# Storing the first attention's normalised rows as f16 high and low halves, and turning those halves in the first expert stage

## The reference

```python
x = x + tanh(g_xattn[0]) * attention(layernorm(x), ctx, ...)      # causal, one head
x = x + tanh(g_ffn[0]) * experts(layernorm(x), Wr, W1, b1, W2, b2, ...)
# experts: 8 experts, 2 per token, at most 640 tokens for each
probs = softmax(xn @ Wr.T); scores, chosen = top_k(probs, 2); scores /= scores.sum(-1)
for e in range(8):
    idx = the first 640 tokens that chose e (and did not overflow earlier)
    y[idx] += (gelu(xn[idx] @ W1[e] + b1[e]) @ W2[e] + b2[e]) * score[idx]
# tokens past an expert's 640 are computed by a fallback network instead
x = x + tanh(g_xattn[1]) * dilated_attention(...)                 # second layer, not touched
x = x + tanh(g_ffn[1]) * expert_choice(...)
```

## Time and profile before

| | us |
|---|---|
| three runs | 849.19, 846.90, 848.25 |
| median | 848.25 |
| the profiled execution | 846.92 |
| span of its instructions | 845.2 |
| mean granted clock of TensorE | 0.869 of full speed |

### The profile page before, as it was taken

One profiled execution on the slowest core, in us unless ns is written; L12 is line 12 of the kernel. 1 busy time (PEld: TensorE's weight loads), 2 busy tenths in 40 slices (PEclk: granted clock), 3 DMA queues, 4 the chain that ended last, 5 costly groups with the idle time before them and its releaser, 6 DMA issues. The chain is left out here.

```text
span 845.2 us, 14866 instructions
## 1 busy us (share of the span) xinstructions
PE 634.7 (75%) x4843; PEld 473.2 (56%) x4843; DVE 513.2 (61%) x1772; ACT 415.3 (49%) x810; POOL 345.8 (41%) x478
## 2 busy tenths in 40 slices
PE   6998898289999999999523778877977730158994
PEld 5787786248768767877411445544544420046773
DVE  1575666666666575564106667779775618866752
ACT  2444431165785686577111466556755611046772
POOL 2433343465347337542312443344533312034754
PEclk9998999679999999999855798889988955569999
DMA  5461233355464455542311222223200014015643
GB/s 162 145 201 51 76 103 123 85 155 145 89 143 105 95 124 113 140 79 27 49 51 32 59 77 65 71 69 91 86 33 28 26 39 150 0 59 145 153 109 38
DMA packets 73873, 75.95 MB, mean 90 GB/s; under 512 B 8037, under 2 KB 66449, under 8 KB 73553
## 3 DMA queue, kind: packets, MB, share of 16 engines
q1 hardware_dynamic: 61217, 59.32, 22.7%
q0 software_dynamic: 10928, 15.57, 11.0%
q10 hardware_dynamic: 1664, 0.27, 0.2%
HBM read 52.20 MB, written 22.94 MB: 89 GB/s over the span
## 5 line engine op out<-in xcount | busy, mean ns | idle before, releaser
L1896 DVE CUSTOM_DVE_ANT_0 c_sn<-c_ps_s,k_mask 128x128 f32<-128x128 f32 (+1 forms) x256 | 75.8, 352 | 55.0 <-PE c_ps_s L2034 54.8
L1420 PE MATMUL b_ps_y<-b_w2h,b_hh 128*128 128x256 f16 x320 | 87.3, 273 | 4.7 <-DVE b_xl L1313 4.4
L1230 POOL DMA_INDIRECT res<-b_y,b_s_idx x40 | 73.4, 1834 | 41.6 <-ACT b_y L1272 31.8
L1728 POOL TENSOR_SCALAR_AFFINE_SELECT c_pr<-c_pr 128x512 f32<-128x512 f32 x64 | 42.8, 669 | 110.0 <-ACT c_pr L1787 109.0
L1420 PE MATMUL b_ps_y<-b_w2h,b_hl 128*128 128x256 f16 x320 | 87.2, 273 | 0.0
L1420 PE MATMUL b_ps_y<-b_w2l,b_hh 128*128 128x256 f16 x320 | 87.2, 273 | 0.0
L1304 DVE TENSOR_TENSOR b_hl<-b_h,b_hh 128x640 f16<-128x640 f32 x64 | 52.9, 826 | 39.2 <-ACT b_hh L1252 39.0
L1216 POOL DMA_INDIRECT e_xg<-rows,e_g_idx x35 | 36.9, 1056 | 83.5 <-DVE e_g_idx L1331 73.0
L2062 PE MATMUL c_ps_v<-c_pr,k_vx 128*64 128x256 f32 (+1 forms) x512 | 64.3, 378 | 5.5 <-POOL c_pr L1728 4.8
L1385 PE MATMUL b_ps_h<-b_xh,e_w1h 128*128 128x320 f16 x256 | 57.1, 305 | 3.1 <-ACT b_h L1247 2.1
L1787 ACT ACTIVATE c_pr<-c_ps_t 128x768 f32<-128x768 f32 x64 | 51.7, 807 | 13.8 <-PE c_ps_t L2048 13.8
(11 more groups left out here) (400 smaller groups left out, 1768.1 us busy)
## 6 DMA issues: line engine op xcount, KB each, us to landing
e_w<-in_L_ffn_W_dram SPq DMA_DIRECT2D x16, 1024.0 KB, 5.5
d_w<-in_L_ffn_W_down_dram SPq DMA_DIRECT2D x8, 640.0 KB
k_ks<-kT SPq DMA_DIRECT2D x48, 64.0 KB, 2.9
c_qs<-q SPq DMA_DIRECT2D x48, 64.0 KB, 2.3
d_w<-in_L_ffn_W_up_dram SPq DMA_DIRECT2D x4, 682.0 KB, 5.3
rows<-a_rows SPq DMA_DIRECT2D x8, 264.0 KB, 2.8
rows<-c_rows SPq DMA_DIRECT2D x8, 264.0 KB, 2.2
a_x_in<-in_x_dram SPq DMA_DIRECT2D x8, 256.0 KB, 3.5
```

Source lines behind the costliest of these rows:

```text
L1230: pool.indirect_dma_start(out=dram["res"], out_offset=bass.IndirectOffsetOnAxis(ap=s_idx[u][:, j:j + 1], axis=0), in_=y[:, j, :], in_offse ...
L1420: last = pe.matmul(ps_y[(j + CT) % 2][:, 0:D], a, b[:, f, :], start=(f == 0 and k == 0), stop=(f == FC - 1 and k == 2))
L1728: pool.affine_select(out=late, in_=late, compare_op=ALU.is_ge, fill=0.0, base=0, pattern=[[0, 2], [0, 2], [1, P]], channel_multiplier=-1). ...
L1896: dve.tensor_tensor_reduce(sn[r][:, a:b], ps_s[:, r, a:b], mask[:, a:b], -1.0, 3.0e38, ALU.add, ALU.min, mx[g % 2][:, q, r, j:j + 1]).then ...
```

## The change

The tile `rows` keeps its size, but its first 256 f32 words of a row now hold 256 f16 high halves and then 256 f16 low halves; the 8 gate weights stay f32. ACT normalises into a new f32 tile `x1n`, copies that to the high half, and POOL subtracts the high half from `x1n` for the low half, in `gates_of`, between the match table and the weighted one-hots. PE turns `x1n` for the router as it turned `rows`. SP's store of the rows waits for both halves in place of the normalised rows. In the expert stage PE turns high and low halves with an f16 identity, two transposes each, into f16 parts of the same bank; ACT copies the high part and DVE copies the low part. The overflow programs add the halves.

```diff
+def row_parts(tile, D):
+    flat = tile[:].bitcast(F16)
+    return flat[..., 0:D], flat[..., D:2 * D]
...
+        x1n = [sb(f"x1n{u}", [P, 2, D]) for u in range(2)]
+        rows_hi, rows_lo = zip(*(row_parts(r, D) for r in rows))
...
             def gathered(g, u):
-                after(sp, s_xn1, g, 0, 2)
+                after(sp, s_rhi, g)
+                after(sp, s_rlo, g)
                 after(sp, s_gate, g, 0, 2)
...
             pool.memset(ident[:], 0.0).then_inc(s_cst, 1)
+            pool.memset(keep["ident16"][:], 0.0).then_inc(s_ecst, 1)
...
+            pool.affine_select(out=keep["ident16"][:], in_=keep["ident16"][:], compare_op=ALU.not_equal, fill=1.0,
+                               base=0, pattern=[[-1, P]], channel_multiplier=1).then_inc(s_ecst, 1)
...
                 landed(pool, s_rst, g, u, 2)
+                after(pool, s_rhi, g)
+                pool.tensor_tensor(rows_lo[u], x1n[u][:], rows_hi[u], ALU.subtract).then_inc(s_rlo, 1)
                 after(pool, s_pg, g, 0, 2)
...
             def residual_normalised(m, v):
+                after(act, s_x1, m, 0, 2)
+                after(act, s_px1, m, 2)
+                after(act, s_rlo, m, 2)
+                normalise(m, s_nmr1, rstd1[v], nmr1[v], x1[v], x1n[v], s_xn1)
                 landed(act, s_rst, m, v, 2)
-                after(act, s_x1, m, 0, 2)
-                normalise(m, s_nmr1, rstd1[v], nmr1[v], x1[v], rows[v], s_xn1)
+                after(act, s_xn1, m, 0, 2)
+                act.activation(rows_hi[v], x1n[v][:], ACT.Copy).then_inc(s_rhi, 1)
...
-                turn(ps_x, rows[u]).then_inc(s_px1, 1)
+                turn(ps_x, x1n[u]).then_inc(s_px1, 1)
...
-        ps_x = [ps_y[k][:, 0:C * P].rearrange("p (c t) -> p c t", c=C) for k in range(2)]
+        x_parts = [[part.rearrange("p (c t) -> p c t", c=C) for part in row_parts(ps_y[k], D)] for k in range(2)]
...
-                        act.activation(xh[v][:, :, j * P:(j + 1) * P], ps_x[j % 2], ACT.Copy).then_inc(s_xh, 1)
+                        act.activation(xh[v][:, :, j * P:(j + 1) * P], x_parts[j % 2][0], ACT.Copy).then_inc(s_xh, 1)
...
                         dve.wait_ge(s_xh, (e + 1) * CT + j + 1)
-                        dve.tensor_tensor(xl[v][:, :, j * P:(j + 1) * P], ps_x[j % 2],
-                                          xh[v][:, :, j * P:(j + 1) * P], ALU.subtract).then_inc(s_xl, 1)
+                        dve.tensor_copy(xl[v][:, :, j * P:(j + 1) * P], x_parts[j % 2][1]).then_inc(s_xl, 1)
...
-                        for c in range(C):
-                            last = pe.transpose(ps_x[j % 2][:, c, :], xg[v][:, j, c * P:(c + 1) * P], ident[:])
+                        for to, part in zip(x_parts[j % 2], row_parts(xg[v], D)):
+                            for c in range(C):
+                                last = pe.transpose(to[:, c, :], part[:, j, c * P:(c + 1) * P], keep["ident16"][:])
                         last.then_inc(s_px, 1)
```

More of the change, by code:

```diff
@@ L256, in attention_causal @@
         s_mr1 = sem("mr1"); s_nmr1 = sem("nmr1")
-        s_xn1 = sem("xn1"); s_px1 = sem("px1"); s_x1T = sem("x1T"); s_plg = sem("plg")
+        s_xn1 = sem("xn1"); s_rhi = sem("rhi"); s_rlo = sem("rlo"); s_px1 = sem("px1"); s_x1T = sem("x1T"); s_plg = sem("plg")
         s_lg = sem("lg"); s_top = sem("top"); s_tix = sem("tix"); s_tixf = sem("tixf"); s_dl = sem("dl")
@@ L408, in _ @@
                       allow_small_or_imprecise_dtypes=True).then_inc(s_ecst, 1)
-            pool.wait_ge(s_ecst, 7)
+            pool.wait_ge(s_ecst, 8)
+            pool.affine_select(out=keep["ident16"][:], in_=keep["ident16"][:], compare_op=ALU.not_equal, fill=1.0,
+                               base=0, pattern=[[-1, P]], channel_multiplier=1).then_inc(s_ecst, 1)
             pool.affine_select(out=tri[:], in_=tri[:], compare_op=ALU.is_ge, fill=0.0, base=0,
@@ L774, in _ @@
             values(2)
-            dve.wait_ge(s_ecst, 8)
+            dve.wait_ge(s_ecst, 10)
             dve.tensor_copy(free[:], one_row[:]).then_inc(s_free, 1)
@@ L1009, in _ @@
             values(4)
-            pe.wait_ge(s_ecst, 8)
+            pe.wait_ge(s_ecst, 10)
             pe.wait_ge(s_ldb1, 16)
@@ L1435, in overflow_programs @@
     fg = sb("f_fg", [P, NT])
-    rows = sb("f_rows", [P, S.ROW]); res = sb("f_res", [P, D])
+    rows = sb("f_rows", [P, S.ROW]); xr = sb("f_xr", [P, D]); res = sb("f_res", [P, D])
     xT = sb("f_xT", [P, C, P]); h = sb("f_h", [P, FC, P])
@@ L1440, in overflow_programs @@
     s_xT = sem("f_xT"); s_ph = sem("f_ph"); s_h = sem("f_h"); s_py = sem("f_py"); s_yb = sem("f_yb")
-    s_y = sem("f_y"); s_new = sem("f_new"); s_store = sem("f_store"); s_passs = sem("f_passs")
+    s_y = sem("f_y"); s_new = sem("f_new"); s_xr = sem("f_xr"); s_store = sem("f_store"); s_passs = sem("f_passs")
     rows_t = dram["rows"].rearrange("(t p) d -> t p d", p=P)
@@ L1481, in on_vector @@
             with dve.Fori(0, NT) as i:
+                dve.wait_ge(s_rows, (i + 1) * 16)
+                hi, lo = row_parts(rows, D)
+                dve.tensor_tensor(xr[:], hi, lo, ALU.add).then_inc(s_xr, 1)
                 dve.wait_ge(s_py, i + 1)
@@ L1494, in on_tensor @@
             with pe.Fori(0, NT) as i:
-                pe.wait_ge(s_rows, (i + 1) * 16)
+                pe.wait_ge(s_xr, i + 1)
                 for c in range(C):
-                    last = pe.transpose(ps_x[:, c * P:(c + 1) * P], rows[:, c * P:(c + 1) * P], ident[:])
+                    last = pe.transpose(ps_x[:, c * P:(c + 1) * P], xr[:, c * P:(c + 1) * P], ident[:])
                 last.then_inc(s_px, 1)
@@ L2674, in build @@
             ("prob", [P, S.NT, S.E]), ("fallen", [P, S.NT]))}
+        keep["ident16"] = ctx.enter_context(nc.sbuf_tensor("ident16", [P, P], F16))
         keep["fallen_n"] = ctx.enter_context(nc.sbuf_tensor("fallen_n", [P, 1], I32))
```

## The result

The changed kernel takes 858.37 us (median of 4 runs) where the kernel before took 847.58 beside it: a ratio of 1.0123, with a 95% interval of 1.0087 to 1.0158. That is 10.8 us slower. The forecast was 856.3, 8.1 slower. Two executions of the kernel before, taken beside hi_alone_filled, both_fill and before_fill_wait, lasted 1276.50 and 3138.58 us and are in no median and no ratio. The profiled executions stand 11.2 apart (858.17 against 846.92, spans 856.4 and 845.2), and these 11.2 are not where the forecast had them. I cut both spans at four points of PE: the first and the last start of the router's logits (line 941, now 959), the first turn of the experts (line 1396, now 1414), and the first and the last start of the second expert product (line 1420, now 1438).

What follows compares the result with a forecast made beforehand. It took the block pipeline as a chain round the engines and the expert stage as PE's own length plus waits. 4.5 + 3.0 + 1.2 + 1.6 + 0 - 2.2 = +8.1 gave 856.3 us, range 850.5 to 861.0.

Steps and rivals of the forecast that it cites:

- its own last test: Forecast called wrong if pipeline start-to-start times don't grow, or the expert stage gains more than 4 us.
- The high half on ACT: Block pipeline: one more copy between normalised rows and exponentials, 0.65 in each of seven blocks, +4.5 us.
- The low half on POOL: Block pipeline: POOL's subtraction holds DVE's gate lines, delaying the residual sum 0.85 in four uncovered blocks; +3.0 us together.
- The clock: Block pipeline: longer PE pauses bring two more falls to the lower clock, 0.8 each, +1.6 us.
- the second rival: Clock falls in every block, also under the scores and the next product; about 859.5 us, chance 0.17.
- The tail: After the pipeline: the last two blocks' subtractions delay POOL's key copies, which hold up DVE's routing loop; +1.2 us.
- f16 transposes: Expert stage: four f16 transposes take the same 0.22 as two f32 ones in each of 40 blocks; 0 us.
- The low part: Expert stage: DVE's copy takes 0.283 where the subtraction took 0.419, saving 0.136 at each of 16 waits; -2.2 us.
- The first rival: DVE isn't held by POOL's subtraction, so terms 3.0 and 1.2 go; 852.1 us, chance 0.15.
- the third: Expert stage: DVE's low-part copy is no faster than the subtraction, 0.419; 858.5 us, chance 0.08.
- the fourth: Expert stage: each f16 transpose costs as much as an f32 one; 865.1 us, chance 0.03.
- the last: Block pipeline has room for the new work, its end set by the loads; 846.0 us or faster, chance 0.05.

Runs made afterwards that it cites:

- hi_alone_filled: Changed kernel with POOL's low-half subtraction moved behind the sum of the weighted one-hots, plus seven unread identity transposes per block in PE's pauses; 849.04 us.
- both_fill: Changed kernel with both half copies moved off their places, three unread transposes before the logits, and POOL's fills behind the first expert's bias copy; 840.86 us.
- before_fill_wait: Kernel before, without halves, plus three unread transposes per block before the logits and POOL's fills behind the first expert's bias copy; 840.86 us.
- hi_after_turn: Changed kernel with ACT's copy to the high half moved behind its copy of the turned rows (x1T); 848.36 us.
- before_fills_wait: Kernel before, with POOL waiting for DVE's copy of the first expert's bias before filling the second attention's tiles; 844.74 us.
- oldturn: Changed kernel with the expert lines undone: f32 transposes, ACT's high part and DVE's subtraction as in the kernel before; 863.82 us.
- the two filled kernels: Unread identity transposes put in PE's pauses: seven per block in the changed kernel, 850.57 us; three per block in the kernel before, 844.43 us.

## Why the forecast was near, and what in it was wrong

The time is 2.1 above the forecast and in its range, and that is in part luck. By its own last test ("if the expert stage gains more than 4 us, which the waits alone don't explain") the account behind it fails: from the first turn to the last product the experts gained 4.7. Two errors of opposite sign met: the blocks cost 3.8 more than forecast, and the experts gave 2.5 more. (PE's first expert turn came at 182.3, where about 178 was expected.)

*The high half on ACT*, +4.5: right. 0.72 a block with the clock up, where 0.65 was taken.

*The low half on POOL*, +3.0: right in kind, too large, and wrong as a term that adds up. The hold costs about 0.5 a block where DVE has nothing else to wait for (0.46, 0.52 and 0.53 in three steps), not 0.85: the forecast let both gate lines run behind the subtraction and put the residual sum 1.51 after the end of the match, but line 705 ends with the subtraction, 706 follows at once, and the sum starts 1.18 after the match (in hi_after_turn line 446 ends at 97.43, and the sum starts at 98.61). And in the changed kernel as it is, the residual sum waits for PE in every block but the first; removing the hold moved no step between logits by more than 0.02 from the second on. The forecast let PE cover it only in the two blocks in which it did so before.

*The clock*, +1.6: the step that failed. I counted two more falls at 0.8; there were four more, as the second rival had it (859.5, chance 0.17). A block with a fall takes 13.70 where one with both halves and a full clock takes 12.57, 1.1 more and not 0.8. What all falls cost can only be estimated. With 1.25 added to each of the seven steps of before_fills_wait (83.8 + 7 x 1.25 = 92.5) they cost 6.6 of the 99.1; with the steps that were read without a fall (13.36 for the first, of the changed kernel, 12.57 five times and 13.11 for the last, of oldturn: 89.3) they cost 9.8. The kernel before has 86.2 - 83.8 = 2.4 of them. So they cost 4 to 7 us more, not 1.6. The argument that "a pause of 1.05 passes today" read a single execution of a kernel whose clock falls twice in one execution and not at all in another. What decides whether it falls I can't settle. That PE's idleness has to do with it, the two filled kernels make likely; that the new pause before the probabilities is the only cause is refuted by hi_after_turn, where that wait is as before and the clock falls.

*The tail*, +1.2: +0.4.

*f16 transposes*, 0: right. At the first expert's turns ACT waits for PE alone (the kernel before, then the changed one):

```profile
168.34 1.11 PE L1396 MATMUL b_ps_y<-ident,e_xg 128*128 128x128 f32 x4 [6.08 <-DMA e_xg<-rows,e_g_idx]
169.07 0.38 ACT L1261 ACTIVATE b_xh<-b_ps_y 128x256 f16<-128x256 f32 x1 [16.55 <-PE b_ps_y L1396]
```

```profile
182.26 1.03 PE L1414 MATMUL b_ps_y<-ident,e_xg 128*128 128x128 f16 x8 [5.56 <-DMA e_xg<-rows,e_g_idx]
182.91 0.38 ACT L1279 ACTIVATE b_xh<-b_ps_y 128x256 f16<-128x256 f16 x1 [15.97 <-PE b_ps_y L1414]
```

ACT starts on the high part 0.73 after the turn's start before and 0.65 after; over these five turns it is 0.67 to 0.73 and 0.64 to 0.67.

*The low part*, -2.2: the copy's price was met to 0.001, but the sum took the saving at all 16 waits, and it came about once for an expert: the steady part of the experts gained 0.8, where seven times 0.135 would be 0.9. Later turns show why (again before, then changed):

```profile
191.09 0.38 PE L1396 MATMUL b_ps_y<-ident,e_xg 128*128 128x128 f32 x2
...
192.30 0.74 ACT L1252 ACTIVATE b_hh<-b_h 128x640 f16<-128x640 f32 x1
192.94 0.37 ACT L1261 ACTIVATE b_xh<-b_ps_y 128x256 f16<-128x256 f32 x1
...
193.81 0.42 DVE L1313 TENSOR_TENSOR b_xl<-b_ps_y,b_xh 128x256 f16<-128x256 f32 x1
...
194.29 0.28 PE L1420 MATMUL b_ps_y<-b_w2h,b_hh 128*128 128x256 f16 x1 [0.58 <-DVE b_xl L1313]
```

```profile
201.07 0.39 PE L1414 MATMUL b_ps_y<-ident,e_xg 128*128 128x128 f16 x4
...
202.45 0.74 ACT L1270 ACTIVATE b_hh<-b_h 128x640 f16<-128x640 f32 x1
203.09 0.37 ACT L1279 ACTIVATE b_xh<-b_ps_y 128x256 f16<-128x256 f16 x1
...
203.96 0.28 DVE L1331 COPY b_xl<-b_ps_y 128x256 f16<-128x256 f16 x1
...
204.30 0.28 PE L1438 MATMUL b_ps_y<-b_w2h,b_hh 128*128 128x256 f16 x1 [0.60 <-DVE b_xl L1331]
```

PE has turned the block nearly 2 us before ACT comes to it: ACT works without a pause here, one high part each 1.73 us in both kernels, and the low part starts 0.87 after the high part in both. From the high part to the second product it is 1.35 before and 1.21 after, so the copy's 0.14 is gained there. But what PE saves at one wait only brings it earlier to the next, which ACT's row ends; its wait before the second product stays (0.58 and 0.60). The forecast read the 16 waits as DVE's and overlooked that ACT sets the pace there.

*The first expert*, which had no term: -3.9. The held copy is most of it: without it the kernel before goes from 26.0 to 23.5, and the kernels with halves lie between 21.9 and 23.0. The rows that foretold it were there, in the trace of the kernel before: a copy of 128x8 that takes 5.08 us beside POOL's fills. I had read that stage by its waits for b_xl and not by its longest instructions.

The first rival (DVE isn't held) is refuted by line 705, the third (a copy of 0.419) by the 0.284, the fourth (dear f16 transposes) by four of them taking 0.39 where the f32 pair takes 0.38, the last (room in the pipeline) by ACT's wait before the normalised rows, which stayed at 0.67 where it had to shrink.

## What to carry to other kernels

An instruction put on the chain that sets a pipeline's period can cost more than its length where the clock falls in its pauses: move it to where its engine waits anyway, which here bought back 10.0 of 10.8 us by the medians (7.3 of 12.9 between the logits) for seven copies of 0.63. Terms that end at the same wait don't add; ask of each whether it still counts when the others are there, and of a saving whether another engine sets the pace. Compare a step only with the same step: the fifth and the sixth here differ by 0.4 us without any change. And look in a stage for tiny instructions with long times: one of 128x8 elements at 5.08 us was worth more than the whole turning.

## What the runs showed of the hardware

- POOL's fills (three of 128x2048 f16, 5.30 us together) held DVE's copy of 128x8 f32 to their end (5.08 us), and the copy took 0.16 where it was over before they began. By the Trainium skill ("SBUF — State Buffer", section "Who interferes with whom") a copy in a two-port mode and a GpSimd instruction exclude each other, whichever issues first; the rows show it for the fills ahead of the copy, and no view shows the copy's mode.
- Transposes that do no work can pay: three per block before the logits made the kernel before 3.4 us faster (0.9939, 0.9905 to 0.9974), with a mean granted clock of 0.871 in place of 0.867.
- The same block code had two stretches at the lower clock in one execution and none in another, 86.2 and 83.8 us for seven blocks.
